# An adaLN block of attention and a quantised FFN: two far products summed by TensorE, dequantising moved to GpSimd, several small TensorE pieces rewritten

## The reference

```
mod = silu(c) @ wmod                      # per batch: sa, ca, ga, sb, cb, gb; the gates at least 0.25 in size
h = layernorm(x) * (1 + ca) + sa
q, k, v = h @ W.T + b                      # 16 heads of 16 channels
scores = where(mask, q.k, 0) / 4           # mask: j = i, and j = i - 2**n for n = 0..8
x = x + ga * (softmax(scores) @ v @ Wo.T + bo)
h = layernorm(x) * (1 + cb) + sb
out = x + gb * (dequant(quant_fp6(h)) @ dequant(quant_fp6(W)).T + bias)   # blocks of 32 channels
```

## Time and profile before

| what | value |
|---|---|
| median of three runs | 286.42 us |
| profiled execution, first to last instruction (its span; the page gives no other time for it) | 285.0 us |
| TensorE busy / VectorE busy | 255.6 us / 258.8 us |
| ScalarE busy / GpSimd busy | 212.5 us / 210.5 us |
| granted TensorE clock | 1.000 over the span |
| chain that ended last, by engine | DVE 39%, POOL 19%, PE 18%, issue 11%, ACT 11% |
| costliest line of that chain | POOL L677, 14% |

### The profile page before, as it was taken

How to read it: one execution, slowest core, us unless ns; L and a number is a source line. 1 busy time by engine, 2 the same in 40 slices (tenths; PEclk the granted TensorE clock), 3 DMA queues, 4 the chain that set the end, 5 groups by cost and what they waited for, 6 DMA issues and landing times.

```text
span 285.0 us, 4442 instructions
## 1 busy us (share of the span) xinstructions
PE 255.6 (90%) x1368; PEld 158.8 (56%) x1368; DVE 258.8 (91%) x326; ACT 212.5 (75%) x577; POOL 210.5 (74%) x152
## 2 busy tenths in 40 slices
PE   6999997697978795989999999999999988997885
PEld 1653554175526561666556646664567646794663
DVE  3699799969995999999999999999999999999970
ACT  2386987975697779879898989887776937575752
POOL 7101439895879999999999999999999699845100
PEclk9999999999999999999999999999999999999999
DMA  7743977694784239724993389347943965730005
GB/s 225 193 181 81 340 248 232 230 338 133 240 273 148 73 125 350 251 72 131 295 336 127 129 263 286 135 113 222 333 147 94 279 198 178 230 103 11 0 26 199
DMA packets 54399, 53.91 MB, mean 189 GB/s; under 512 B 4100, under 2 KB 52824, under 8 KB 54376
## 3 DMA queue, kind: packets, MB, share of 16 engines
q1 hardware_dynamic: 54376, 53.63, 60.1%
HBM read 44.90 MB, written 8.72 MB: 188 GB/s over the span
## 4 chain that ended last, share of the span: by engine, by line
DVE 39%; POOL 19%; PE 18%; issue 11%; ACT 11%; DVEq 0%; POOLq 0%; ACTq 0%
POOL pv_buf L677 14%; DVE prod L1721 9%; DVE pv_buf L1851 9%; DVE prod L1851 4%; DVE prod L1710 4%; PE ps L988 3%; PE ps L1067 3%; PE ps L826 2%; ACT dump L1197 2%; PE ps L853 2%; ACT dump L1238 1%; DVE ps L1825 1%; PE ps L837 1%; DVE ps L1827 1%; POOL rstd L658 1%
## 5 line engine op out<-in xcount | busy, mean ns | idle before, releaser
L677 POOL TENSOR_TENSOR pv_buf<-pv_buf 128x1024 f32<-128x1024 f32 (+2 forms) x60 | 132.5, 2209 | 15.0 <-DVE pv_buf L1851 9.8
L1721 DVE TENSOR_TENSOR prod<-ps,kT 128x1024 f32<-128x1024 f32 (+4 forms) x70 | 75.1, 1110 | 0.0
L1851 DVE TENSOR_TENSOR pv_buf<-v_shift,ps 128x1024 f32<-128x1024 f32 x49 | 59.1, 1212 | 0.0
L937 PE MATMUL ps<-prod,sel_sum 128*32 128x512 f32 x256 | 30.8, 598 | 8.5 <-DVE prod L1721 7.8
L853 PE MATMUL ps<-wT,h_cen 128*128 128x256 f32 x128 | 29.9, 379 | 0.0
L826 PE MATMUL ps<-hT,wT 128*128 128x512 f32 x64 | 29.7, 596 | 0.0
L837 PE MATMUL ps<-hT,wT 128*128 128x512 f32 x64 | 29.3, 599 | 0.0
L988 PE MATMUL ps<-wo_g,w_raw 128*128 128x256 f32 x112 | 27.9, 392 | 0.0
L853 PEld LDWEIGHTS ps<-wT,h_cen 128*128 128x128 f32 x128 | 23.9, 190 | 6.4 <-issue 3.8
L988 PEld LDWEIGHTS ps<-wo_g,w_raw 128*128 128x128 f32 x112 | 20.1, 189 | 5.4 <-issue 3.2
L937 PEld LDWEIGHTS ps<-prod,sel_sum 128*32 128x32 f32 x256 | 6.7, 109 | 28.0 <-issue 13.8
(11 more groups left out here) (212 smaller groups left out, 550.3 us busy)
## 6 DMA issues: line engine op xcount, KB each, us to landing
v_shift<-v_rows SPq DMA_DIRECT2D x56, 512.0 KB, 5.7
x_in<-in_L_attn_x SPq DMA_DIRECT2D x8, 512.0 KB, 4.4
v_rows<-v_base SPq DMA_DIRECT2D x8, 512.0 KB, 4.1
x_res<-in_L_attn_x SPq DMA_DIRECT2D x8, 512.0 KB, 6.5
out_x<-outb SPq DMA_DIRECT2D x5, 512.0 KB, 5.8
rows_mod<-mod_rows SPq DMA_DIRECT2D x7, 256.0 KB, 3.4
x<-in_L_wmod SPq DMA_DIRECT2D x1, 1024.0 KB, 7.9
row_ga<-mod_rows SPq DMA_DIRECT2D x8, 128.0 KB, 4.9
```

The lines of the kernel that those rows point to most:

```text
L677: nc.gpsimd.tensor_tensor(dst, dst, ring(b, n)[:, t:NT, :], ALU.add).then_inc(s_add, 1)
L937: mm = nc.tensor.matmul(ps23[32 * g:32 * g + 32, 1, :], sel_sum[:, which, c, :], prod[:, n, c, :], start=(c == 0 and which == 0), stop=(c ...
L1721: nc.vector.tensor_tensor(prod[:, n, :, o:L], ps01[:, :, o:L], kT[:, b % 2, :, 0:L - o], ALU.mult).then_inc(s_prod, 1)
L1851: nc.vector.tensor_tensor(dst[:, t:NT, :].rearrange("p t (h e) -> p t h e", e=DH), v_n.rearrange("p t (h e) -> p t h e", e=DH), weights, A ...
```

## The change

It does these things:

1. Products 8 and 9 (`FAR`) of batches 0 to 5 go to buffers of their own (`far_buf`), and TensorE adds them: `attention_transposes` turns their three and two tiles into the same PSUM banks ahead of the sum's four. GpSimd's `add(b, 8)` and `add(b, 9)` go; `NADD` is 7. The transposes wait for `s_d` of batch b + 1, VectorE's far products for the transposes of the batch before.
2. `dequantise` of batches 0, 1 and 2 leaves VectorE (passes 3, 4 and 5) and becomes `dequantise_early` on GpSimd, between `gate_ffn(b - 3)` and `add(b, 1)`. ScalarE's copy of its scale to PSUM (L1428) goes.
3. The bias matmuls take 128 rows, of which 125 are zero, instead of 3. Two memsets on GpSimd clear the rest once.
4. The far scores are turned with a permutation matrix (four transposes) instead of multiplied with a folding matrix (eight passes).
5. The means of v are taken for batches 0 to 2, 3 to 5 and 6 to 7 together, with as many columns, into another bank, and ScalarE reads them three times instead of eight.
6. `dump`, which nothing reads, is bf16.

```diff
-    NADD = NO - 1
+    FAR = [n for n in range(NO) if OFFS[n] >= P]
+    NADD = NO - 1 - len(FAR)
...
-            def dequantise_fourth():
-                b = LAST - 3
+            def dequantise_early(b):
                 pool.wait_ge(s_q8, b + 1)
                 pool.wait_ge(s_xd, b)
                 pool.wait_ge(s_post, NPOST * (b + 1))
                 nc.gpsimd.tensor_tensor(xd[:, :, :].rearrange("p t (g k) -> p (t g) k", k=BLOCK),
                                         q8[:, :].rearrange("p (g k) -> p g k", k=BLOCK),
-                                        over(mx_scale[:, :], BLOCK), ALU.mult).then_inc(s_xd, 1)
+                                        over(block_scales(b)[1][:, :], BLOCK), ALU.mult).then_inc(s_xd, 1)
...
                 if has(b - 3):
                     gate_ffn(b - 3)
+                    dequantise_early(b - 3)
...
                 add(b, 7)
-                add(b, 8)
-                add(b, 9)
...
             def attention_transposes(b):
-                pe.wait_ge(s_vm, b + 1)
+                pe.wait_ge(s_vm, means_of(b) + 1)
+                pe.wait_ge(s_d, b + 2)
...
-                pe.wait_ge(s_add, NADD * (b + 1))
-                for t in range(NT):
+                for i, n in enumerate(FAR[::-1] + [0]):
+                    if n == 0:
+                        pe.wait_ge(s_add, NADD * (b + 1))
+                    else:
+                        pe.wait_ge(s_pv, NO * b + n + 1)
+                    part = product_tiles(b, n)
+                    for t in range(tiles_of(n), NT):
...
-                    mm = nc.tensor.matmul(ps[:, t // 2, col:col + 3 * HEADS], s2_sb[:, P * t:P * t + P], fold[:, :],
-                                          start=True, stop=True, skip_group_check=True)
+                    mm = nc.tensor.transpose(ps[:, t // 2, col:col + P], s2_sb[:, P * t:P * t + P], fold[:, :])
...
-                nc.tensor.matmul(ps[:, half_, :].rearrange("p (t c) -> p t c", c=D), ones3[at:at + NSPLIT, 0:P],
-                                 bias_ffn[at:at + NSPLIT, b % 2, :].unsqueeze(1).broadcast_to([NSPLIT, 2, D]),
+                nc.tensor.matmul(ps[:, half_, :].rearrange("p (t c) -> p t c", c=D), ones3[:, 0:P],
+                                 bias_ffn[:, b % 2, :].unsqueeze(1).broadcast_to([P, 2, D]),
...
-                if 0 <= b - 3 < TAIL - 1:
-                    act.wait_ge(s_post, NPOST * (b - 2) - 1)
-                    nc.scalar.activation(step_scale, kept_scale[:, :], ACT.Copy).then_inc(s_kept, 1)
...
-                if has(b - 1):
-                    mean_of_v(b - 1)
+                if b in (1, 4):
+                    means_of_v(means_of(b - 1))
...
                 pv_product(b, 3)
-                if has(b - 3):
-                    dequantise(b - 3)
                 qk(b, 2, 3)
```

More of the change, by code:

```diff
@@ L358, in block_scales, with means_of, mean_at @@
             return tail_amax, tail_scale[:, b - TAIL - 2], tail_inv[:, b - TAIL - 2]
-        def mean_at(b):
-            return (ps67[:, 1], VM + NC * (b % 2)) if b < LAST - 1 else (ps23[:, 0], NC * (b % 2))
+        def means_of(b):
+            return next(i for i, group in enumerate(MEANS) if b in group)
+        def mean_at(group, c):
+            n = len(MEANS[group])
+            return ps23[:, 0, n * c:n * c + n]
         def tiles_of(n):
@@ L597, in _ @@
             nc.gpsimd.memset(v_shift[:, 0, 0, :], 0.0).then_inc(s_const, 1)
[L598 to L601, removed]
+            nc.gpsimd.tensor_copy(fold[:, :].rearrange("p (y x h) -> p y x h", x=4, h=HC),
+                                  ident[:, :].rearrange("p (x y h) -> p y x h", x=4, h=HC)).then_inc(s_const, 1)
             def split_gated_biases():
@@ L725, in _ @@
             gate_ffn(LAST - 3)
[L726 removed]
+            dequantise_early(LAST - 3)
             add(LAST - 1, 3)
@@ L889, in attention_transposes @@
                     pe.wait_ge(s_z, b - 1)
-                pe.wait_ge(s_add, NADD * (b + 1))
-                for t in range(NT):
[L892 to L895, removed]
+                for i, n in enumerate(FAR[::-1] + [0]):
+                    if n == 0:
+                        pe.wait_ge(s_add, NADD * (b + 1))
[3 more added lines that the diff above has]
+                    for t in range(tiles_of(n), NT):
+                        for c in range(NC):
+                            mm = nc.tensor.matmul(ps67[:, c, P * t:P * t + P],
+                                                  part[:, t - tiles_of(n), P * c:P * c + P], ident[:, :],
+                                                  start=(i == 0 and t == tiles_of(n)), stop=(n == 0 and t == NT - 1),
+                                                  is_transpose=True, skip_group_check=True)
                 mm.then_inc(s_attp, 1)
@@ L900, in summed_attention @@
                 pe.wait_ge(s_prod, NO * B)
-                parts = [(ring(b, n), n) for n in PE_SUMMED] + [(pv_buf[:, b % 2], 0)]
-                for i, (part, n) in enumerate(parts):
+                parts = PE_SUMMED + [0]
+                for i, n in enumerate(parts):
+                    part = product_tiles(b, n)
                     pe.wait_ge(s_pv, NO * b + n + 1)
@@ L1526, in _ @@
             exps(LAST - 1)
-            mean_of_v(LAST - 2)
             evacuate_v(LAST, 1)
```

135 lines of the change are left out of this document (70 added, 65 removed).

## The result

| | before | after |
|---|---|---|
| median | 287.06 us (14 runs, 286.42 to 289.52) | 289.21 us (14 runs, 288.08 to 290.40) |
| ratio | 1 | 1.0069, 95% interval 1.0046 to 1.0093 |
| profiled execution, span | 285.0 us | 286.9 us |
| TensorE / VectorE busy | 255.6 / 258.8 us | 250.5 / 254.7 us |
| ScalarE / GpSimd busy | 212.5 / 210.5 us | 209.9 / 198.0 us |

The account below looks back on a forecast made before the run. The bound was a full loop of waits through GpSimd and ScalarE, 29.55 us a pass. softmax_weights(6) 2.4 us late, less 0.5 at the end, gave net 1.9 on 286.42: 288.3 us, range 285.3 to 289.8.

Parts of the forecast that it names:

- GpSimd's loop and dequantising in series: GpSimd's 23.86 us from modulate to rstd hand-over, then ScalarE's norms and exps; dequantising ahead of add 1 adds 1.87 a pass.
- Adds 8 and 9 beside ScalarE gain nothing in the loop: End of GpSimd's pass: removing some 3.3 us of adds gains nothing in a full pass, as ScalarE's path ends 0.03 later.
- TensorE does not become the bound: TensorE per pass: transposes +1.3 at most, means -0.9, far scores -0.5, four biases 0.25 less each; sum -1.1 us.
- the VectorE rival: VectorE's passes: VectorE is the bound and its saved work gains 4.5 us, giving 281.9 us; chance 0.16.
- -0.9: TensorE per pass: saving in us claimed from mean passes gone in four of six passes.
- The sign to look for: VectorE idle ahead of softmax_weights of 4 and 5, some 1.5 and 3 us, released by ScalarE's exps.
- The late-fp8 rival: Ten transposes ahead of evacuate_attention delay quantised; GpSimd waits 0.9 us in each of three passes, 291.0 us; chance 0.05.
- Padding's price: TensorE's bias matmuls at 128 rows: 0.25 us gained each, two at the kernel's end giving 0.5 back.
- The rival that padding brings nothing: Bias matmuls at the end: 128 rows gain nothing, the 0.5 us is not given back, 288.8 us; chance 0.14.
- the 0.23 us of cover: GpSimd before dequantising: fp8 values there 5.75 us after modulate starts, gate_ffn ends at 5.98, so waiting costs nothing.
- the lead forecast: Pass 2: hand-over 0.3 us earlier (0 to 0.6), modulate(1) at 122.8, 0.6 early.

## Why the prediction was right or wrong

- **GpSimd's loop and dequantising in series: right.** Alone it gives 31.42 us a pass against 31.42 worked out. In the kernel after, pass 4 has 31.07 against 25.73 + 5.41 = 31.14.
- **Adds 8 and 9 beside ScalarE gain nothing in the loop: right.** GpSimd's idle 3 us stand where they stood.
- **"TensorE does not become the bound", -1.1 us a pass: this step failed.** It added up TensorE's work and didn't ask where each piece stands, the very fault found in the VectorE rival. The ten transposes stand in a loop of TensorE and ScalarE that was as full as GpSimd's (29.7 us), and cost 1.09 us a pass there. The means that were taken away (1.02 us at 145.87) had stood beside ScalarE's copies of the scores; TensorE now idles there for 1.55 us, so their -0.9 was no gain, and in pass 3, where they are taken for three batches, they stand behind the scores and cost 0.81. The sign to look for was there: VectorE was to wait 1.5 and 3 us for ScalarE's exps in passes 3 and 4, and it waits 1.11 and 1.26 for them, but 1.61 and 1.36 before that for TensorE's scores. The late-fp8 rival named these transposes, and looked for their effect on GpSimd only.
- **Hence the attribution was half wrong.** In the kernel after two loops lie side by side: GpSimd's takes 32.03 us from pass 3 to 4 (with the late fp8 and the means) and 31.07 from 4 to 5, TensorE and ScalarE's 31.21 and 30.32. Moving dequantising costs 3.4 us alone, but taking it back from the change returns only 0.86 of 3.06 us in the profiles. The time came out right because the second loop, though missed, is 0.8 us a pass shorter than the first and lies beside it: loops side by side don't add. That was luck, as nothing in the prediction had its length.
- **Padding's price: mis-sized.** Per half 0.30 instead of 0.25, 0.60 at the end; the other 0.9 of the 1.48 us in the tail come from VectorE's instruction, which nobody had priced. The rival that padding brings nothing was wrong, since the gain is in the gaps between the loads and not in their length. The LDWEIGHTS section of the Trainium skill's page TensorE: Matmul & The Clock Gate says that 32 rows load as long as 128. The trace agrees on the duration (0.09 us with 3 rows, 0.10 with 128).
- **fp8: the 0.23 us of cover was gone in pass 3,** and GpSimd waited 0.64. Counted from the 0.33 us by which this execution was late from the start, `modulate(1)` began 0.65 earlier than before, the lead forecast, but the fp8 values came 0.21 later (129.70 against 129.16), because of TensorE's delay with the clock down. So the lead was eaten by the wait. Passes 4 and 5 had no wait. `softmax_weights(6)` came 3.38 late instead of 2.4: 0.64 of it this, 0.33 the place at which the execution already stood at 41 us. The tail gave back 1.48 instead of 0.5. Two misses of a microsecond cancelled, and that is luck too.
- **VectorE's gain** needed 28.6 us passes; in the kernel after no pass with the FFN in it was under 30 (VectorE's maxima at 118.18, 148.43, 179.65, 211.22).

## What to carry to other kernels

Where three engines are near nine tenths, look for every closed loop of waits and write down its length: a change costs what it adds to the longest, and undoing it returns only the distance to the next one. Ask of each added instruction where it stands, also when the engine's total falls. Work taken out of a place beside another engine is worth nothing until the hand-over is moved past it, and here moving `rstd` ahead of one add and splitting one wait did that.

## What the runs showed of the hardware

- A VectorE instruction with both inputs in SBUF is held off by one of GpSimd that began before it. In all fourteen profiled executions `kT<-x_norm,rows_mod` ended 1.07 to 1.09 us after GpSimd's `wT<-wT,row_gb`, whenever it had itself begun: it took 2.22 us where it began 0.13 behind GpSimd (before), 1.58 at 0.77 behind (dequantising back), 1.31 at 1.04 behind (only the bias rows). VectorE's `pv_buf<-v_shift,ps`, with one input in PSUM, isn't held: it took 1.21 in the midst of GpSimd's adds (in the kernel after at 133.66, the adds from 131.64 to 141.57). The Trainium skill, SBUF — State Buffer, section SBUF: two separate sides, calls this an exclusive lock for the whole of the first instruction. The trace agrees.
- TensorE's clock falls from the higher to the lower of its two levels (2.4 and 1.2 GHz) behind some idle times and not behind others of the same length: the kernel before idled up to 2.77 us and stayed at 1.00 in its profile, while the one with dequantising back fell behind 1.97 us (the 16 sums took 2.94 us instead of 1.92) and again behind 3.12 (0.52 from 110 to 115 us).
- A weight load of 3 rows between loads of 128 is not set close to its neighbours: 0.31 us from the bias to the first pass behind it with 3 rows (277.25 to 277.56), 0.21 to 0.22 with 128 (278.84 to 279.05 with the bias rows alone).
